# The up product of a routed feed-forward with its operands exchanged: weights stationary, rows moving

## The reference, cut to what matters

```
scores = xn @ w_router.T                        # 8 experts
_, ids = top_k(scores, 2); c = softmax(scores) at ids
h  = xn @ w_up[e].T                             # 1408 columns: 704 value, 704 gate
h  = val * silu(gate)
y  = h @ w_down[e].T                            # 704 -> 256
out = sum over the two experts of c * y, + skip
```

## Time and profile before

| | us |
|---|---|
| median of 3 runs | 443.6 (439.12 to 444.65) |
| the profiled execution | 439.83 |
| its span, first to last instruction | 438.0 |
| stage E's first up matmul starts | 184.0 |
| its last down matmul starts | 426.4 |

### The profile page before, as it was taken

The page is one execution under the profiler, slowest core; times in us unless marked ns, Lnnn a source line. Parts: engine busy times, 40 slices in busy tenths (PEclk is TensorE's granted clock), DMA queues, the critical chain, the costliest instruction groups (busy, mean ns, idle before and its releaser), DMA issues.

```text
span 438.0 us, 9733 instructions
## 1 busy us (share of the span) xinstructions
PE 365.9 (84%) x2444; PEld 263.8 (60%) x2445; DVE 269.9 (62%) x688; ACT 236.5 (54%) x434; POOL 191.2 (44%) x186
## 2 busy tenths in 40 slices
PE   0899999788996411289999999999999999999980
PEld 0678888677885311056666666666666666666650
DVE  3698879978788899854445544455444554445530
ACT  3699877876765660534453444444445344444430
POOL 2544445866667413214333443334433444433321
PEclk9999999999998555599999999999999999999996
DMA  8999943352213170224343433434334343343420
GB/s 237 399 426 403 347 134 97 96 193 73 72 49 96 49 198 0 49 49 53 61 75 61 73 60 61 73 61 73 58 63 73 61 73 60 61 72 61 62 24 12
DMA packets 45859, 47.02 MB, mean 107 GB/s; under 512 B 26256, under 2 KB 41616, under 8 KB 44816
## 3 DMA queue, kind: packets, MB, share of 16 engines
q1 hardware_dynamic: 38304, 36.28, 26.5%
q0 software_dynamic: 7536, 10.52, 15.0%
HBM read 32.17 MB, written 9.50 MB: 95 GB/s over the span
## 4 chain that ended last, share of the span: by engine, by line
PE 70%; DVE 12%; issue 4%; ACT 4%; DMA 4%; SPq 1%; POOL 1%; DVEq 0%; ACTq 0%; POOLq 0%
PE bank L1225 32%; PE bank L1251 5%; PE bank L1276 5%; PE bank L1277 5%; PE bank L1278 5%; PE bank L1105 3%; PE bank L1153 3%; PE bank L1162 2%; DMA expert_w<-in_wup 2%; PE bank L1117 2%; ACT arena L438 2%; DVE expert_w L827 2%; DVE expert_w L836 1%; DVE arena L982 1%; PE bank L1058 1%
## 5 line engine op out<-in xcount | busy, mean ns | idle before, releaser
L1225 PE MATMUL bank<-expert_w,arena 128*128 x702 | 153.5, 364 | 8.8 <-DMA arena<-arena 8.6
L726 POOL DMA_INDIRECT out<-arena,add_idx x39 | 61.7, 1583 | 132.4 <-ACT arena L602 132.4
L1225 PEld LDWEIGHTS bank<-expert_w,arena 128*128 128x128 f16 x702 | 67.5, 98 | 68.0 <-issue 12.6
L1021 DVE COPY arena<-bank 128x1024 f16<-128x1024 f16 x39 | 27.0, 692 | 55.4 <-PE bank L1251 55.3
L620 ACT ACTIVATE arena<-arena 128x512 f16<-128x512 f32 x39 | 24.6, 630 | 64.8 <-DVE arena L1035 64.8
L1035 DVE SCALAR_TENSOR_TENSOR arena<-bank,dn_small,arena 128x512 f32<-128x512 f32 x78 | 45.4, 582 | 21.2 <-PE bank L1225 17.3
L1276 PE MATMUL bank<-expert_w,arena 128*128 x195 | 53.2, 273 | 1.3 <-DVE arena L1021 0.9
L1277 PE MATMUL bank<-expert_w,arena 128*128 x195 | 53.2, 273 | 0.0
L1278 PE MATMUL bank<-expert_w,arena 128*128 x195 | 53.2, 273 | 0.0
L716 POOL DMA_INDIRECT arena<-xrow_hbm,take_idx x39 | 38.9, 998 | 24.5 <-issue 11.5
L1041 DVE TENSOR_TENSOR arena<-arena 128x512 f16<-128x512 f32 x39 | 27.0, 693 | 27.1 <-ACT arena L620 27.1
(11 more groups left out here) (176 smaller groups left out, 673.5 us busy)
## 6 DMA issues: line engine op xcount, KB each, us to landing
expert_w<-in_wup SPq DMA_DIRECT2D x8, 1408.0 KB, 17.1
expert_w<-in_wdn SPq DMA_DIRECT2D x10, 640.0 KB, 5.0
rows<-in_x SPq DMA_DIRECT2D x8, 256.0 KB, 7.0
arena<-in_ctxT SPq DMA_DIRECT2D x8, 256.0 KB, 3.1
xrow_hbm<-front SPq DMA_DIRECT2D x8, 256.0 KB, 2.2
out<-rows SPq DMA_DIRECT2D x8, 256.0 KB, 2.8
expert_w<-in_wdn SPq DMA_DIRECT2D x20, 64.0 KB, 4.9
cst_b<-in_consts_b SPq DMA_DIRECT2D x1, 960.0 KB, 12.4
```

What stands on the lines that cost most here:

```text
L726: pool.indirect_dma_start(out=out, in_=yt[:, i % 2], in_offset=None, out_offset=bass.IndirectOffsetOnAxis(ap=add_idx[:, i:i + 1], axis=0), ...
L1225: last = T.matmul(bank[q][:, 0:n], xsT[:, slot, 2 * a + c], up_w[:, ds(w0 + c * UPC + w * 2 * H + lo, n)], start=m == 0, stop=m == len(pro ...
```

## The change

The up product holds a 128x128 piece of the weights stationary and streams the 128 rows of a piece of `xsT`. The result, and so `hh`, has h columns on partitions, which is what the down product takes as its stationary operand. The 11 transposes and the two copies from PSUM go; ACT writes the high half and DVE the low half straight into `hT`, which has two slots, as the up banks (0 to 2, 3 to 5) and the y bank (6, 7) now have. 704 is five tiles of 128 and one of 64, so the last 384 columns (192 gates, 192 values) are taken as three stationary pieces of every third column, and the down weights of h rows 512 to 703 are loaded by every third row to match: 9 DMAs for an expert and not 3. `load_down` moves behind the stores in SP's `step_b`. On PE a step is now the whole up product of tile i, then the down product of tile i-1.

```diff
@@ arena views
-        sg = view(arena, 1728, H)
-        hh = view(arena, 2432, H)
-        hT = view(arena, 3136, H).bitcast(fp16).rearrange("p (c n) -> p c n", c=NHS)
+        sg = view(arena, 1728, HA + 3 * P)
+        hh = view(arena, 1728 + HA + 3 * P, NH * P)
+        hT = view(arena, 1728 + HA + 9 * P, 2 * H).bitcast(fp16).rearrange("p (s c n) -> p s c n", s=2, c=NHS)
+        hT_low = [hT[:, s, NH:NHS].rearrange("p c n -> p (c n)") for s in range(2)]
+        hT_high = [hT[:, s, 0:NH].rearrange("p c n -> p (c n)") for s in range(2)]
...
@@ SP
             def load_down(e, place, landed):
-                tail = place * DNC + (NH - 1) * D
-                sp.dma_start(dn_raw[:, place * DNC:tail], wdn[e][:, 0:(NH - 1) * D]).then_inc(landed, 16)
-                for lo in (0, HLAST):
-                    sp.dma_start(dn_raw[lo:lo + HLAST, tail:tail + D], wdn[e][0:HLAST, (NH - 1) * D:DNC]).then_inc(landed, 16)
+                at_c = place * DNC
+                sp.dma_start(dn_raw[:, at_c:at_c + 4 * D], wdn[e][:, 0:4 * D]).then_inc(landed, 16)
+                for j, lo, c in ((0, 0, 4), (1, HLAST, 4), (2, 0, 5), (2, HLAST, 5)):
+                    n = (P - j + 2) // 3
+                    dst = dn_raw[lo:lo + HLAST, at_c + c * D:at_c + (c + 1) * D]
+                    sp.dma_start(dst[0:n], wdn[e][j:P:3, 4 * D:5 * D]).then_inc(landed, 16)
+                    sp.dma_start(dst[n:HLAST], wdn[e][(j + 1) % 3:HLAST:3, 5 * D:DNC]).then_inc(landed, 16)
...
@@ ACT, step_e
-                    nc.scalar.activation(hT[:, 8:NHS], hT_bank[1], ACT.Copy).then_inc(s_hTb, 1)
...
-                    nc.scalar.activation(hs_high[:, 0:HA], hh[:, 0:HA], ACT.Copy).then_inc(s_hhi, 1)
+                    nc.scalar.activation(hT_high[slot][:, 0:HA], hh[:, 0:HA], ACT.Copy).then_inc(s_hhi, 1)
...
-                    nc.scalar.activation(sg[:, HA:H], bank[2][:, 0:HB], ACT.Silu, scale=descale2[:, ds(e, 1)]).then_inc(s_sg, 1)
+                    nc.scalar.activation(sg[0:HLAST, HA:HA + 3 * P], bank[3 * slot + 2][0:HLAST, 0:3 * P], ACT.Silu,
+                                         scale=descale2[0:HLAST, ds(e, 1)]).then_inc(s_sg, 1)
...
@@ DVE, step_e
-                    V.tensor_copy(hT[:, 0:8], hT_bank[0]).then_inc(s_hTa, 1)
...
+                    V.scalar_tensor_tensor(out=hh[0:HLAST, HA:HA + 2 * P], in0=bank[3 * slot + 2][HLAST:P, 0:2 * P],
+                                           scalar=h_scale[0:HLAST, ds(e_h, 1)], in1=sg[0:HLAST, HA:HA + 2 * P],
+                                           op0=ALU.mult, op1=ALU.mult)
+                    V.scalar_tensor_tensor(out=hh[HLAST:P, whole], in0=bank[3 * slot + 2][HLAST:P, 2 * P:3 * P],
...
@@ PE
-            def up(i, slot, w0, q, lo, n, between=None):
+            def up_tile(q, slot, w0, t, columns):
                 for m, (c, a, w) in enumerate(products):
-                    last = T.matmul(bank[q][:, 0:n], xsT[:, slot, 2 * a + c],
-                                    up_w[:, ds(w0 + c * UPC + w * 2 * H + lo, n)],
-                                    start=m == 0, stop=m == len(products) - 1)
-                last.then_inc(s_up, 1)
+                    last = T.matmul(bank[3 * slot + q][:, t * P:(t + 1) * P], columns(w0 + c * UPC + w * 2 * H),
+                                    xsT[:, slot, 2 * a + c], start=m == 0, stop=m == len(products) - 1)
+                return last
+
+            def whole(lo):
+                return lambda w0: up_w[:, ds(w0 + lo, P)]
+
+            def every_third(j):
+                return lambda w0: up_w[:, ds(w0 + 2 * HA, 2 * HB)].rearrange("p (n t) -> p t n", t=3)[:, j]
...
-                    up(i, slot, w_up, 0, 0, HA)
+                    for q in range(2):
+                        for t in range(HA // P):
+                            last = up_tile(q, slot, w_up, t, whole(q * HA + t * P))
+                        last.then_inc(s_up, 1)
+                    if live(r, 2, NSLOT):
+                        load_expert("down", at(it, k, 2)[0], 2 * DNC)
+                    for t, columns in enumerate((every_third(0), every_third(2), every_third(1))):
+                        last = up_tile(2, slot, w_up, t, columns)
+                    last.then_inc(s_up, 1)
                 if live(r, 2, NSLOT):
-                    for c in range(NHS):
-                        last = T.transpose(hT_bank[c // 8][:, c % 8], hs[:, c * P:(c + 1) * P], ident16[:, :])
-                    last.then_inc(s_trh, 1)
...
+                    y = bank[6 + slot][:, 0:D]
```

More of the change, by code:

```diff
@@ L394, in step_b @@
                     load_ctx(b, slot)
[L395 to L400, removed]
                 if r == NBATCH:
@@ L410, in step_b @@
                     sp.dma_start(out[ds(b * SEQ, SEQ), :].rearrange("(j p) n -> p j n", p=P), rows[:, ds(b * 2, 2), :]).then_inc(s_out0, 16)
+                if r < NE - 4:
+                    load_down(r + 2, r + 2, s_dnw[r + 2])
+                if r == NE - 4:
+                    sp.wait_ge(s_sqd, 2)
+                    for e in range(NE - 2, NE):
+                        load_down(e, e, s_dnw[e])
             steps(sp, step_b, B_STEPS[0], B_STEPS[0], B_STEPS[0])
@@ L601, in step_e @@
                         act.wait_ge(s_add, 16 * i - 16)
-                    nc.scalar.activation(yt[:, slot], bank[7][:, 0:D], ACT.Copy, scale=pair_scale[:, ds(i, 1)]).then_inc(s_yt, 1)
+                    nc.scalar.activation(yt[:, slot], bank[6 + slot][:, 0:D], ACT.Copy, scale=pair_scale[:, ds(i, 1)]).then_inc(s_yt, 1)
                 if live(r, 1, NSLOT):
@@ L1005, in _ @@
             V.tensor_copy(descale2, descale).then_inc(s_ysc, 1)
+            V.memset(hh[HLAST:P, (NH - 1) * P:NH * P], 0.0)
             down_low(DN_TABLE, DN_GATHER)
@@ L1027, in step_e @@
                 if live(r, 1, NSLOT):
[L1029 to L1035, removed]
-                                               op0=ALU.mult, op1=ALU.mult).then_inc(s_h, 1)
-                        dve.wait_ge(s_hhi, 2 * i + q + 1)
-                        if r >= 2 and q == 0:
-                            dve.wait_ge(s_trh, i)
-                        if q == 0:
-                            V.tensor_tensor(hs_low, hh[:, cols], hs_high[:, cols], ALU.subtract).then_inc(s_hlo, 1)
-                        else:
-                            V.tensor_tensor(hs_low4, hh[:, HA:HA + P], hs_high[:, HA:HA + P], ALU.subtract)
-                            V.tensor_tensor(hs_low_tail, hh[:, HA + P:H], hs_high[:, HA + P:H], ALU.subtract).then_inc(s_hlo, 1)
@@ new lines, in step_e @@
+                    i, _, slot = at(it, k, 1)
+                    tail = slice((NH - 1) * P, NH * P)
+                    whole = slice(HA, (NH - 1) * P)
+                    dve.wait_ge(s_sg, 2 * i + 1)
+                    dve.wait_ge(s_up, 3 * i + 2)
+                    if r >= 2:
+                        dve.wait_ge(s_hlo, 2 * i - 1)
+                    V.scalar_tensor_tensor(out=hh[:, 0:HA], in0=bank[3 * slot + 1][:, 0:HA], scalar=h_scale[:, ds(e_h, 1)],
+                                           in1=sg[:, 0:HA], op0=ALU.mult, op1=ALU.mult).then_inc(s_h, 1)
@@ new lines, in step_e @@
+                    V.scalar_tensor_tensor(out=hh[HLAST:P, whole], in0=bank[3 * slot + 2][HLAST:P, 2 * P:3 * P],
+                                           scalar=h_scale[0:HLAST, ds(e_h, 1)], in1=sg[0:HLAST, HA + 2 * P:HA + 3 * P],
+                                           op0=ALU.mult, op1=ALU.mult).then_inc(s_h, 1)
+                    dve.wait_ge(s_hhi, 2 * i + 2)
+                    V.tensor_tensor(hT_low[slot][:, whole], hh[:, whole], hT_high[slot][:, whole], ALU.subtract)
+                    V.tensor_tensor(hT[HLAST:P, slot, NH - 1], hh[0:HLAST, tail], hT[0:HLAST, slot, NH - 1],
+                                    ALU.subtract).then_inc(s_hlo, 1)
```

83 lines of the change are left out of this document (26 added, 57 removed).

## The result

The changed kernel takes 571.5 us (median of 4 runs, 569.4 to 572.2), the kernel before 442.8 in the same comparison: ratio 1.291, 95% interval 1.282 to 1.301. The forecast was 553 with a range of 522 to 590; direction, mechanism and range hold, the size is 18.5 us short. The profiled execution took 572.21 us, its span 570.4. The kernel before took 438.1 to 440.1 us in 17 of the 22 executions timed beside e8 and e9 and 441.7 to 443.4 in the five with a lower mean granted clock, so a difference of 1 to 3 us between two medians can be nothing but the mix of the two.

The account below looks back on a forecast made before the run. The array's columns bound the kernel before; after the change PE's sequencer would. Profiled 439.8 + 109.8 (stage E) + 2 (stage B) = 551.6, predicted as 553 us because the runs' median is 3.8 above that execution; range 522 to 590.

Parts of the forecast that it names:

- The array after the change: Stage E: PE's array would need 5.56 us a tile, 0.48 less, at 56 ns per pair of load and matmul.
- The sequencer becomes the bound: Stage E: address instructions rise from 24 to 56 a tile, so PE's sequencer needs 9.0 us against the array's 5.56.
- The price, 0.124, and the rest, 1.3 + 0.8: Sequencer budget per tile: 0.124 us per address instruction, 1.3 for two expert-number reads, 0.8 for waits and half a branch.
- The matmuls ride along: PE's sequencer: address instructions stand equally far apart with one or two matmuls between them, so matmuls add nothing.
- Stage B, +2, at most +5: Stage B: 18 small down loads delay batch 5's context on SP's queue; +2 us, bounds 0 and +5.
- main case: Whole kernel: the sequencer bounds stage E, 553 us, with 540 to 575 as its own range; chance 77%.
- the array as the bound: Rival, stage E: address instructions hidden or few, so the array stays the bound; 19 us less, 421 us; chance 5%.
- Code fetched again: Rival, stage E's loop: longer body fetched at each turn, +15 to +48, 568 to 601 us; chance 9%.
- The clock in stage E: Rival, stage E: PE's clock falls to 1.2 GHz, 11.1 us a tile, 632 us; chance 4%.
- The parts overlapping: Rival, stage E: reads and waits run beside address instructions, 6.94 us a tile, 474 us; chance 5%.
- The gain itself: Stage E: if the array's saving were all, 39 tiles x 0.48 = 19 us gained.

Follow-up runs that it names:

- e8: Kernel before, with the read of the expert's number moved from the middle of a down product to its end: 438.1 us against 439.6.
- e9: Kernel before with e8's move, and the loop's second down product reusing the number read for the up product (three reads per two tiles): 441.0 us.
- e1: Changed kernel with the up product's weight addresses fixed to expert 0, removing 44 address instructions a tile: 444.5 us.
- e3: Kernel before with its up matmuls cut into pieces of 128 columns, operands not exchanged and transposes kept: 570.2 us.
- e2: Changed kernel with weight addresses fixed to expert 0 in the first of three up parts alone, removing 16 address instructions a tile: 509.0 us.
- e4: Kernel before with its up matmuls cut into pieces of 256 columns, 36 address instructions a tile: 471.1 us.
- e6: Changed kernel with load_down back ahead of the stores and the down rows laid out so an expert's load is one DMA: 559.1 us.
- e7: Kernel before with the changed kernel's down loads alone, 9 DMAs an expert, behind the stores: 452.7 us against 439.4.
- e10: e6 with e1's edit: changed kernel with one-DMA down loads ahead of the stores and up addresses fixed to expert 0: 430.7 us.

## Why the prediction was right, step by step

- **The array after the change** (5.56 us a tile, 56 ns a pair): right. e1 shows 56 ns for 66 pairs in a row and 5.64 from start to start. The Trainium skill's 81 ns ("TensorE: Matmul & The Clock Gate", Back-to-back issue gap) is not what the runs show, neither with nor without strided weights.
- **The sequencer becomes the bound**: right, and shown from both sides: without the address instructions the loss goes (e1), with them and without the exchange it comes (e3).
- **The price, 0.124, and the rest, 1.3 + 0.8**: the mis-sized term of stage E. The price is 0.128 in the mean: most distances are 0.124, and about one in ten is 0.03 to 0.05 longer. 39 x 56 x 0.004 = 9 us, which is the stage's whole miss of 8.9 (118.7 for 109.8). The rest came out as 9.27 - 56 x 0.128 = 2.1, as forecast. I had read the price from ten instructions in one stretch; over all of stage E the trace before has a mean of 0.127. What makes the longer ones longer is open.
- **"The matmuls ride along"**: true behind an address instruction, and so here. Elsewhere they cost about 15 ns a pair (e2), which is why e2 to e4 came out 10 to 17 us above what I expected of them.
- **Stage B, +2, at most +5**: the step that failed. It was 12, outside its own bounds, and the loads are behind 12 to 13 us in the medians (e6, e7). The wait for batch 5's context was named, with its place, but sized 2.6 where 4.7 came: SP took 9.9 us for the 18 loads, as worked out, but a context load took 6.0 us to land (median; 3.1 before) with the small loads ahead of it. Not seen at all: the wait for batch 2's context, which the 36 early loads in SP's queue delay; the half clock behind the 4.7 us, worth some 1.7; and the first stretch of half clock, worth some 3.5, which is not the loads' alone. The prediction put the 1.81 us of one issue down to a full queue; no run shows that, and the same load behind the same two stores took 0.51 us one batch earlier.
- **Behind stage E**: nothing was forecast, 1.7 us came. With 8.9 of stage E and 10 of stage B this makes up the 20.6 us between the sum, 551.6, and the profiled execution, 572.2. The bounds of the main case, 540 to 575, were set for the price of an address instruction; that they covered stage B's miss as well is luck.
- **Rivals: the array as the bound**: not so, the sequencer's budget was what it seemed.
- **Code fetched again**: no. The packets on that queue went from 8 to 12, for a longer program, so the sign that the prediction gave, more than 8, came without its rival: the last two ahead of the loop's first branch (256.4) start at 242.8 and 252.5, the next at 541.7, behind its last branch (535.8). The prediction's note that two lines of 16 KiB would not hold the changed loop goes too far. In the tiles written out ahead of the loop a block of 16 KiB is fetched every 10 us or so, and a tile of 9.3 us has 235 instructions with the loads, so a block holds some 250, and two would about hold the loop's 470. But e3's loop has 517, and once it has turned for the first time it goes through fifteen more turns without a fetch. There the trace agrees with the 128 KiB that the Trainium skill ("Runtime: NRT & Kernel Launch", Instruction fetch mechanics) gives PE, and not with its two lines of 16 KiB, if by little.
- **The clock in stage E**: no, 0.99 with the array fed two thirds of the time in the up product.
- **The parts overlapping**: no, 56 x 0.128 alone would be 7.2 and not 9.27. e1's 12 address instructions and the changed kernel's 56 differ by only (9.27 - 5.97) / 44 = 0.075 each because e1 is bound by the array; between e2 and the changed kernel it is the full price, once the 0.4 us of e2's bare pairs are counted.
- **The gain itself**: 19 us were forecast for the array alone; with both losses out (e10) it is 9. A tile has 5.91 us there and not 5.74: from one last down matmul to the next it is 5.54 in every second tile, the array's time as worked out, and about 6.1 in the others, where reads, waits and the loop's branch show even with 12 address instructions. That leaves 12 us of the 19 in stage E (230.4 for 242.7). Another 3 go behind it, 14.3 us from the last matmul to the end for 11.3: the last three additions to the output each wait for the one before.

## What to carry to other kernels

An engine's sequencer has a budget of its own, and the page's busy table does not show it: count, for each tile, the instructions that set an address from a register, times the distance between two of them on the timeline of that engine, and compare with the engine's own time for the tile. Cutting a long matmul with a run-time address into short ones multiplies these instructions while the array's work stays the same; exchanging the operands did so by itself, since the weights had moved in pieces of 512 and 384 columns and now stand still in pieces of 128. And a load that becomes many small ones on a shared queue has to be followed to whatever is issued behind it, and from there to the clock.

## What was not expected of the hardware

- An address instruction stands 46 ns in its row and is 124 ns from the next, whether one pair of load and matmul stands between them or two; 128 in the mean over stage E. Two with no pair between them are 104 ns apart.
- Loads of 128 columns with a step of 3 elements and contiguous ones are the same: 66 pairs at 56 ns (e1).
- A pair without an address instruction before it costs the sequencer some 15 ns (0.4 us for 24 in e2).
- A 4.7 us wait of PE in stage B was followed by 3.5 us at half clock (0.51); holes of 0.4 to 0.9 us in every tile of stage E left it at 1.00.
- The same instructions in stage B ran at half clock for 0, 3.4 and 6.8 us in the profiled executions of three kernels (before, e8, e9) that differ in stage E alone.
